# Clamp in the PSUM bank, a store in four parts, GpSimd's maxima in other places, unread TensorE products in three waits of a two-layer cross-attention kernel

## Chip, cores and metric

The kernel runs on one core of a Trainium2 chip. Its time is the device time of one execution in microseconds (us); less is better.

## What is computed

x is (16, 100, 256), the context (16, 361, 192). Four blocks each add to x what they make of layernorm(x):

```python
x = x + L0_xattn(layernorm(x), ctx)   # 16 heads of 16; scores clipped at +-1e4, softmax, PV, Wo
x = x + L0_ffn(layernorm(x))          # top-2 of 8 experts, capacity 500, plus 0.1 * a shared FFN
x = x + L1_xattn(layernorm(x), ctx)   # ternary weights, int8 activations
x = x + L1_ffn(layernorm(x))          # a recurrent cell over 16 steps
```

In L1_xattn every linear layer scales its input by the maximum of its absolute value over the whole tensor, so nothing can be multiplied before that one number is known:

```python
i_scale = jnp.maximum(jnp.max(jnp.abs(x)), 1e-08) / 127.0
qx = jnp.clip(jnp.round(x / i_scale), -128.0, 127.0)
```

There are six such maxima: of the context (CTX), of vis, the first linear layer's output (VIS), of the image embeddings (IMG_), of the normalised text (TEXT), of the concatenation (CAT) and of the hidden layer (HID).

## The kernel before

Every engine has its own stream, written out by hand in `@block.vector`, `@block.gpsimd`, `@block.scalar`, `@block.tensor` and `@block.sync` (from L2452); the order in each is fixed, and they meet by semaphores alone. There is no planner.

**Attention (L540 to L818).** `over_batches` (L988) walks 16 batches, the middle ones in a hardware loop. Each batch b has eight steps i, two heads each. TensorE (`a_tensor`, L657) issues in step i the transposed scores of batch b (L549), the plain scores of batch b + 1 (L530), and by turns the key (L378), value (L476), query (L412) and output (L621) products of other batches and the probability-value product (L577). DVE (`a_vector`, L735) takes the score maximum per query (L535), and clips the exponentials of ScalarE (L556) in L565. The maxima of eight heads at a time, a half, go to the other side of the scores as two extra rows: DVE clamps them from SBUF to SBUF (`m_vector`, L499), TensorE transposes them into a free part of bank 6 (`m_tensor`, L504), ScalarE copies the upper 16 bits out (`m_scalar`, L510), DVE the rest (`m_low`, L514), and SP stores them (L521). Half 1 of batch b is clamped and transposed in step 0, half 0 of batch b + 1 in step 4; the copies follow in steps 1 and 5, ahead of ScalarE's exponential, and there TensorE waits for L514 before L577, which writes into the same bank. In the opening, `m_vector` stands behind the maximum of i = HALF - 1 (L2475).

**Experts (L1178 to L1485).** SP stores the outputs of each expert to DRAM when its four parts are done (`expert_store`, L1480, semaphore `ys_out`): 500 KB. With the last one there, GpSimd fetches two rows per token and batch by 32 indirect transfers (L2532), and DVE adds them to x (`combine_vector`, L2111).

**Second layer (L1920 to L2211).** `lin_tensor` (L1712) makes vis and the image embeddings, evicted by ScalarE (L1735) and in part by DVE; DVE takes maxima (L1749), `quant_max` (L1585) joins them in `cmax`, GpSimd takes the maximum over the partitions (`quant_gpsimd`, L1590, PARTITION_ALL_REDUCE), and DVE turns it into scales (`quant_scale`, L1574). GpSimd has VIS's maximum behind the gathers of batch 2 (L2535). The normalised text is transposed (L210), copied to xnT by ScalarE (L2082), reduced (L2162), scaled and multiplied (L1930); then the small attention (L1763), after which CAT's maximum holds up the product L1944, and HID's the product L1977. Between these two, GpSimd prepares the recurrent cell's weights (`cell_weights_gpsimd`, L2338), the last part of them behind HID's maximum.

## Time and profile before

| | |
|---|---|
| median of 3 runs | 927.25 us (925.16 to 928.35) |
| the profiled execution | 924.2 us, of which the span from first to last instruction is 922.4 |
| busy of the span | TensorE 84%, VectorE (DVE) 77%, ScalarE (ACT) 61%, GpSimd (POOL) 33% |
| attention / experts / second layer / cell | up to about 333 / 624 / 839 / 922 us |
| mean granted TensorE clock | 0.921 of 2.4 GHz |

PE is TensorE's matmul, PEld its weight load, SPq a transfer issued by SP. Every instruction stands under the line of the kernel that issued it. "Idle before" is the time its engine stood still ahead of it, with the engine that released it as the trace infers from semaphores; "issue" means that the profile shows nothing it waited for. Buffers that share one area of SBUF (vis, image, hidden layer, text) all appear as `area`. The granted clock has two levels, 1.0 (2.4 GHz) and 0.5 (1.2 GHz); a value between them in a window is their mean over time.

### The profile page before, as it was taken

The numbers are of one execution on the slowest core, as the hardware profiler recorded it, in microseconds if no ns is written. First come the engines' busy times: TensorE is split into PE (matmuls) and PEld (weight loads), VectorE is DVE, ScalarE is ACT, GpSimd is POOL, SyncE is SP. The second block draws the span as 40 slices with busy tenths as digits, with TensorE's granted clock in tenths as the row PEclk, the third lists the DMA queues.
The fourth block names the chain that finished last, engine by engine and source line by source line (L and its number), as shares of the span: only waits on it lengthen the run. The fifth ranks groups of instructions, "written<-read, shape, count | busy, mean of one in ns | idle before, by whom it ended". The sixth has DMA issues, their size and how long they took to land.

```text
span 922.4 us, 21748 instructions
## 1 busy us (share of the span) xinstructions
PE 779.0 (84%) x8198; PEld 581.1 (63%) x8198; DVE 710.6 (77%) x1453; ACT 558.3 (61%) x1155; POOL 305.5 (33%) x254
## 2 busy tenths in 40 slices
PE   3688999999997786999899999996626999769994
PEld 2456666666665573778477777783214877459994
DVE  7779889888887896875677777637786988777766
ACT  6667677677764356443655556647957776763542
POOL 6235646555453442040522220004730221442400
PEclk9799999999999668899999999998657999889997
DMA  6434444445543447141477766521210000200002
GB/s 173 110 89 102 111 106 103 107 108 125 137 107 82 134 139 243 66 136 49 127 198 195 193 191 176 151 72 54 76 46 0 2 1 1 92 0 2 3 1 72
DMA packets 75271, 89.60 MB, mean 97 GB/s; under 512 B 22054, under 2 KB 61761, under 8 KB 75194
## 3 DMA queue, kind: packets, MB, share of 16 engines
q1 hardware_dynamic: 68362, 80.50, 31.6%
q0 software_dynamic: 6144, 7.42, 3.3%
q8 instruction: 49, 0.80, 0.4%
q10 hardware_dynamic: 688, 0.66, 0.3%
q14 instruction: 28, 0.23, 0.1%
HBM read 72.87 MB, written 15.43 MB: 96 GB/s over the span
## 4 chain that ended last, share of the span: by engine, by line
PE 47%; DVE 27%; ACT 12%; issue 8%; DMA 3%; POOL 1%; SPq 1%; DVEq 0%; another core or an unknown queue 0%; ACTq 0%
PE ps L1215 11%; PE ps L1202 9%; DVE p L565 4%; DVE m L535 3%; PE ps L378 3%; PE ps L549 3%; PE ps L476 2%; ACT area L1735 2%; PE ps L2282 2%; PE ps L577 2%; PE ps L530 2%; DVE m32c L499 2%; PE ps L2293 2%; DVE pmax L1749 1%; ACT area L2104 1%
## 5 line engine op out<-in xcount | busy, mean ns | idle before, releaser
L535 DVE TENSOR_REDUCE m<-ps 100x2 f32<-100x722 f32 x128 | 115.0, 899 | 38.6 <-PE ps L530 37.9
L556 ACT ACTIVATE p<-ps 128x800 f32<-128x800 f32 x128 | 106.8, 834 | 48.9 <-PE ps L549 46.8
L1264 ACT ACTIVATE hT<-ps,cols 128x500 f32<-128x500 f32 (+1 forms) x96 | 62.5, 651 | 99.7 <-PE ps L1202 91.5
L1271 DVE TENSOR_TENSOR hT_l<-hT,hT_h 128x500 f16<-128x500 f32 (+1 forms) x96 | 62.5, 652 | 58.6 <-ACT hT_h L1265 56.5
L1215 PE MATMUL ps<-w_h,hT_h 128*125 128x256 f16 (+1 forms) x384 | 105.0, 274 | 1.8 <-DVE x L1311 1.2
L565 DVE SCALAR_TENSOR_TENSOR p<-p 128x600 f32<-128x600 f32 x128 | 105.6, 826 | 0.7 <-ACT p L556 0.7
L1215 PE MATMUL ps<-w_h,hT_l 128*125 128x256 f16 (+1 forms) x384 | 105.0, 273 | 0.0
L1215 PE MATMUL ps<-w_l,hT_h 128*125 128x256 f16 (+1 forms) x384 | 105.0, 273 | 0.0
L1107 POOL DMA_INDIRECT xe<-tokens,slot_of x32 | 42.4, 1326 | 152.5 <-PE ps L1225 102.1
L1202 PE MATMUL ps<-xe_h,w_h 128*128 128x500 f16 (+1 forms) x192 | 72.6, 378 | 17.0 <-ACT hT_h L1265 7.2
L1202 PE MATMUL ps<-xe_l,w_h 128*128 128x500 f16 (+1 forms) x192 | 72.2, 376 | 0.0
L1202 PE MATMUL ps<-xe_h,w_l 128*128 128x500 f16 (+1 forms) x192 | 71.8, 374 | 0.0
L549 PE MATMUL ps<-qs,ks 128*128 128x100 f16 x768 | 62.8, 211 | 6.7 <-ACT p L556 4.2
L396 POOL TENSOR_TENSOR kp<-k,kp 128x361 f16<-128x361 f32 x32 | 46.0, 1437 | 62.3 <-ACT kp L392 62.3
L530 PE MATMUL ps<-ks,qs 128*100 128x361 f16 x256 | 61.8, 324 | 3.9 <-DMA qs<-q_parts 3.1
L549 PEld LDWEIGHTS ps<-qs,ks 128*128 128x128 f16 x768 | 49.9, 99 | 22.6 <-ACT p L556 10.4
L1265 ACT ACTIVATE hT_h<-ps,cols 128x500 f16<-128x500 f32 (+1 forms) x96 | 62.1, 647 | 0.0
L1215 PEld LDWEIGHTS ps<-w_h,hT_h 128*125 128x125 f16 (+1 forms) x384 | 51.1, 133 | 6.5 <-DVE hT_l L1271 1.4
L577 PE MATMUL ps<-p,v 128*32 128x100 f32 (+1 forms) x1536 | 47.9, 258 | 7.0 <-DVE mT L514 3.6
L1215 PEld LDWEIGHTS ps<-w_l,hT_h 128*125 128x125 f16 (+1 forms) x384 | 51.1, 133 | 2.7
L1215 PEld LDWEIGHTS ps<-w_h,hT_l 128*125 128x125 f16 (+1 forms) x384 | 51.1, 133 | 0.0
L577 PEld LDWEIGHTS ps<-p,v 128*32 128x32 f32 (+1 forms) x1536 | 33.7, 112 | 26.5 <-issue 11.4
(353 smaller groups left out, 2107.1 us busy)
## 6 DMA issues: line engine op xcount, KB each, us to landing
stage<-in_ctxT_dram SPq DMA_DIRECT2D x16, 541.5 KB, 6.4
sw<-in_L_ffn_w_dram SPq DMA_DIRECT2D x16, 512.0 KB
sw<-in_L_ffn_w_dram SPq DMA_DIRECT2D x8, 1024.0 KB, 6.0
k_parts<-kp SPq DMA_DIRECT2D x32, 192.0 KB, 3.3
ks<-k_parts SPq DMA_DIRECT2D x32, 192.0 KB
stage<-in_L_xattn_W_f_dram SPq DMA_DIRECT2D x6, 1024.0 KB, 7.0
ctx_f<-in_ctxT_dram SPq DMA_DIRECT2D x16, 270.8 KB, 3.2
ks<-k_parts SPq DMA_DIRECT2D x32, 96.0 KB
```

What stands on the lines that cost most here:

```text
L396: g.tensor_tensor(kp[:, 1, c, 0:KV], k32[c][:, :], kp[:, 0, c, 0:KV], ALU.subtract).then_inc(k_l, 1)
L530: mm = pe.matmul(bank[at + n][0:T, 0:KV], qs[p][:, h, :], ks[p][:, h, 0:KV], start=True, stop=True)
L535: v.tensor_reduce(m32[p][:, 2 * i:2 * i + 2], ps[0:T, at:at + 2, 0:KV], AX.X, ALU.max).then_inc(m_max, 1)
L549: mm = pe.matmul(bank[t_bank(i) + n][:, j * T:(j + 1) * T], keys, qs[p][:, h, :], start=(j == 0), stop=True, skip_group_check=True)
L556: s.activation(p32[:, i % HALF, :, :, :].rearrange("p j n t -> p n j t"), ps[:, t_bank(i):t_bank(i) + 2, 0:(KJ + 1) * T].rearrange("p n (j ...
L565: v.scalar_tensor_tensor(probs, probs, 1.0, low, ALU.min, ALU.max).then_inc(a_cv, 1)
L577: i = pe.matmul(OB_[HR * r:HR * (r + 1), g * T:(g + 1) * T], v32[p][0:m, j, h, :], p32[0:m, h // 2 % HALF, j, h % 2, :], start=(g == 0 and ...
L1202: i = pe.matmul(bank[2 + f % 2][:, 0:width(n)], w1p[ww][:, k, f * 128:(f + 1) * 128], xep[p][xx][:, k, 0:width(n)], start=(k == 0 and ww = ...
L1215: i = pe.matmul(bank[4 + j % 3][0:m, 0:C], hTp[p][hh][:, f, j * m:(j + 1) * m], w2p[of][ww][:, f, :], start=(f == 0 and hh == ww), stop=(f ...
L1264: s.activation(hT[:, f % 3, 0:m], bank[2 + f % 2][:, 0:m], ACT.Silu, bias=bias, scale=1.0 / WS)
L1265: s.activation(hTp[p][0][:, f, 0:m], bank[2 + f % 2][:, 0:m], ACT.Silu, bias=bias, scale=1.0 / WS).then_inc(f_s, 1)
L1271: v.tensor_tensor(hTp[p][1][:, f, 0:m], hT[:, f % 3, 0:m], hTp[p][0][:, f, 0:m], ALU.subtract).then_inc(f_l, 1)
```

## The change

- The clamp moves behind the transposition: TensorE transposes the maxima as they are, DVE clamps the eight rows in the bank, in place, and ScalarE waits for that. In DVE's order the clamp now stands behind the score maximum of its step. TensorE waits for the maxima and for the previous half's L514.
- The last expert's output is stored in four transfers, each when its part is done; the waits for `ys_out[1]` count them.
- GpSimd takes VIS's maximum behind the gathers of batch 4 rather than 2.
- The text maximum is taken in four parts rather than two.
- TensorE runs products that nobody reads: 10 of 512 columns in bank 0 before the text product, 18 in bank 2 after the small attention, 20 in bank 0 after L1944.
- ScalarE computes one unread Exp after the text evictions.
- GpSimd takes two unread maxima over the partitions (of TEXT's `cmax`), one ahead of CAT's and one ahead of HID's.

```diff
         def m_vector(v, b, p, half):
-            v.wait_ge(m_max, NP * b + HALF * (half + 1))
-            wait(v, m_mm, 2 * b + half)
-            v.tensor_scalar(m32c[:, :], m32[p][:, half * NP:(half + 1) * NP], CLAMP, -CLAMP, ALU.min, ALU.max
-                                   ).then_inc(m_c, 1)
-        def m_tensor(pe, b, half):
-            pe.wait_ge(m_c, 2 * b + half + 1)
-            pe.transpose(MT_, m32c[:, :], ident[0:T, 0:T]).then_inc(m_mm, 1)
+            v.wait_ge(m_mm, 2 * b + half + 1)
+            v.tensor_scalar(MT_, MT_, CLAMP, -CLAMP, ALU.min, ALU.max).then_inc(m_c, 1)
+        def m_tensor(pe, b, p, half):
+            pe.wait_ge(m_max, NP * b + HALF * (half + 1))
+            wait(pe, m_l, 2 * b + half)
+            pe.transpose(MT_, m32[p][:, half * NP:(half + 1) * NP], ident[0:T, 0:T]).then_inc(m_mm, 1)
         def m_scalar(s, b, half):
-            s.wait_ge(m_mm, 2 * b + half + 1)
+            s.wait_ge(m_c, 2 * b + half + 1)
...
         def a_vector(v, b, t, p):
             for i in range(NP):
-                if i == 0:
-                    m_vector(v, b, p, 1)
-                if i == 4 and has(b, 1):
-                    m_vector(v, b + 1, q, 0)
...
                     s_vector(v, b + 1, q, i, 2 * (i % 2))
                 else:
                     guard_flag_vector(v, i)
+                if i == 0:
+                    m_vector(v, b, p, 1)
+                if i == 4 and has(b, 1):
+                    m_vector(v, b + 1, q, 0)
...
         def expert_store(q, e, p):
+            if isinstance(e, int) and e == E - 1:
+                for j in range(4):
+                    q.wait_ge(f_y, 4 * (e + NG) + j + 1)
+                    q.dma_start(slots_y[e][:, j, :], ye[p][:, j, :]).then_inc(ys_out[p], 16)
+                return
...
+        def keep_running(pe, at, n):
+            for i in range(n):
+                pe.matmul(at, w_q[F1][:, 0, 0:128], w_q[F1][:, 1, 0:512], start=True, stop=True)
         def layer2_tensor(pe):
...
             ln_tensor(pe, 2)
+            pe.wait_ge(ln_ev, 2 * (B // 2) + 1)
+            keep_running(pe, bank[0], 10)
...
             att_tensor(pe)
+            keep_running(pe, bank[2], 18)
...
                 i.then_inc(h_mm, 1)
+            pe.wait_ge(h_ev, 8 + 4 * FC - 7)
+            keep_running(pe, bank[0], 20)
             pe.wait_ge(h_ev, 8 + 4 * FC)
...
                 if b == B // 2 - 1:
-                    s.wait_ge(ys_out[1], 16 * (E // 2 + 1))
+                    s.wait_ge(ys_out[1], 16 * (E // 2 + 4))
...
+            s.activation(avg_q[0:T, 1, 0:1], eps_col[:, :], ACT.Exp)
             s.wait_ge(pad_set, 1)
             att_scalar(s)
...
-            for h in range(2):
-                v.wait_ge(ln_ev, 2 * (B // 2) + (h + 1) * B // 4)
-                i = v.tensor_reduce(pmax[:, h:h + 1], xnT[:, :, h * NTOK // 2:(h + 1) * NTOK // 2], AX.XY, ALU.max,
-                                    apply_absolute_value=True)
+            for h in range(4):
+                v.wait_ge(ln_ev, 2 * (B // 2) + (h + 1) * B // 8)
+                i = v.tensor_reduce(pmax[:, h:h + 1], group_of(h), AX.XY, ALU.max, apply_absolute_value=True)
             vs.inc(i)
-            quant_max(v, TEXT, 2)
+            quant_max(v, TEXT, 4)
...
+            g_.partition_all_reduce(avg_q[:, 1, 2:3], cmax[:, TEXT:TEXT + 1], 128, RMAX)
             quant_gpsimd(g_, [HID])
...
-                if i == HALF - 1:
+                if i == HALF:
                     m_vector(v, 0, 0, 0)
...
-                g.wait_ge(ys_out[p], 16 * (E // 2 + 1))
+                g.wait_ge(ys_out[p], 16 * (E // 2 + 1 + 3 * p))
             for b in range(B):
...
-                if b == 2:
+                if b == 4:
                     quant_gpsimd(g, [VIS])
             quant_gpsimd(g, range(IMG_, TEXT + 1))
             att_gpsimd(g)
+            g.partition_all_reduce(avg_q[:, 1, 1:2], cmax[:, TEXT:TEXT + 1], 128, RMAX)
             quant_gpsimd(g, [CAT])
```

## Rows read from the trace of the kernel before

**Rows 1.** Windows: stretch, length, busy PE, PEld, DVE, ACT, POOL, then PEclk, DMA share, GB/s.

```profile
165.00:198.00 33.00, 31.14 (x453) 22.07 (x452) 29.34 (x43) 23.30 (x54) 19.54 (x14) 1.00 0.42 105
```

**Rows 2.** L499's own view, and the view of waits (total us, times, longest).

```profile
L499 DVE TENSOR_SCALAR m32c<-m x32: 158/800/1012, 39.8 to 299.6; 100x8 f32<-100x8 f32 x32
...
PE ps L504 <- DVE m32c L499: 13.6, 23, 2.1
```

**Rows 3.** Timeline around one clamp: start us, us, engine, line, operation, [idle before <-releaser].

```profile
211.62 1.77 POOL L650 TENSOR_TENSOR ctxl<-ctx_f,ctxh 96x361 f16<-96x361 f32 x1
...
212.37 0.47 PE L530 MATMUL ps<-ks,qs 128*100 128x361 f16 x2
...
212.58 0.84 DVE L499 TENSOR_SCALAR m32c<-m 100x8 f32<-100x8 f32 x1
...
213.48 0.25 PE L504 MATMUL ps<-const,m32c 100*8 100x100 f32 x1 [0.64 <-DVE m32c L499]
...
214.85 0.24 DVE L514 TENSOR_TENSOR mT<-ps,mT 8x100 f16<-8x100 f32 x1
...
215.35 0.72 PE L577 MATMUL ps<-p,v 128*32 128x100 f32 x24
```

**Rows 4.** Chain of waits: one product per batch (start us, us, what).

```profile
199.26 1.42 PE ps L476 x12
...
216.08 1.42 PE ps L476 x12
...
232.34 0.76 PE ps L476 x6
```

**Rows 5.** Timeline of the second layer's head: store, gathers, a maximum, ScalarE's last halt.

```profile
624.30 0.27 SPq L1482 DMA_DIRECT2D slots_out<-ye  x1
...
631.37 1.23 POOL L2532 DMA_INDIRECT xn<-slots_out,back  x1 [77.89 <-PE ps L1727]
...
641.93 0.35 POOL L1593 PARTITION_ALL_REDUCE gmax<-cmax  x1 [2.75 <-DVE cmax L1588]
...
642.46 1.04 POOL L2532 DMA_INDIRECT xn<-slots_out,back  x1 [0.17 <-issue]
...
676.49 1.07 POOL L2532 DMA_INDIRECT pick_more<-slots_out,back  x1 [0.30 <-issue]
...
679.75 0.65 ACT L1735 ACTIVATE area<-ps,cols,oscale 128x361 f32<-128x361 f32 x1 [2.03 <-PE ps L1727]
```

**Rows 6.** Timeline of GpSimd and DVE around the last two global maxima.

```profile
781.45 0.73 POOL L1996 TENSOR_TENSOR x<-x,f_b 100x256 f32<-100x256 f32 x1 [3.54 <-DVE area L1881]
...
788.58 0.15 DVE L1577 TENSOR_SCALAR iscale<-gmax 128x1 f32<-128x1 f32 x1 [3.71 <-POOL gmax L1593]
...
796.84 5.91 POOL L2344 TENSOR_SCALAR fused<-area 128x512 f16<-128x512 f32 x4 [8.29 <-issue]
...
811.46 1.48 POOL L2349 TENSOR_SCALAR area<-area 128x512 f16<-128x512 f32 x1
...
819.20 0.15 DVE L1577 TENSOR_SCALAR iscale<-gmax 128x1 f32<-128x1 f32 x1 [3.56 <-POOL gmax L1593]
```

**Rows 7.** Windows of 2 us in the second layer, columns as in rows 1.

```profile
786.00:788.00 2.00, 0.00 (x0) 0.00 (x0) 0.00 (x0) 0.00 (x0) 0.00 (x0) 0.68 0.96 320
...
792.00:794.00 2.00, 2.00 (x9) 0.94 (x8) 1.67 (x5) 1.02 (x2) 0.00 (x0) 0.61 0.08 27
...
824.00:826.00 2.00, 2.00 (x19) 2.00 (x18) 0.00 (x0) 1.98 (x3) 0.00 (x0) 0.93 0.00 0
```

**Rows 8.** Timeline of TensorE: first products after three idlings of the second layer.

```profile
699.47 5.49 PE L1930 MATMUL ps<-area,wq_txt 128*128 128x400 f16 x16 [5.46 <-ACT area L2088]
...
790.12 23.48 PE L1944 MATMUL ps<-area,wq_f 128*128 128x400 f16 x128 [6.67 <-ACT area L2100]
...
821.42 8.55 PE L1977 MATMUL ps<-wq_f,area 128*100 128x256 f16 x64 [7.81 <-ACT area L2108]
```

**Rows 9.** Timeline of DVE: the two text maxima.

```profile
693.81 3.54 DVE L2162 TENSOR_REDUCE pmax<-xnT 128x1 f32<-128x1600 f32 x2
```

More of the change, by code:

```diff
@@ L268, in build @@
         m32 = [sba(f"m32_{p}", [T, H]) for p in range(2)]
-        m32c = sba("m32c", [T, H // 2, 2])[:, :, 0]
         mT = sba("mT", [H // 2, 2, 2, T], F16)
@@ L670, in a_tensor @@
                 if i == 0:
-                    m_tensor(pe, b, 1)
+                    m_tensor(pe, b, p, 1)
                 if i == 0 and has(b, 2):
@@ L692, in a_tensor @@
                 if i == 4 and has(b, 1):
-                    m_tensor(pe, b + 1, 0)
+                    m_tensor(pe, b + 1, q, 0)
                 if i == 4 and has(b, 3):
@@ L2641, in _ @@
                 if i == HALF:
-                    m_tensor(pe, 0, 0)
+                    m_tensor(pe, 0, 0, 0)
                 if i == 0:
```

## The prediction, made before the change was run

> **What bounds the kernel now.** I read the chain that ended last first, then the stretches that it names, in time order. No engine bounds the whole; three regimes matter here. In the attention loop TensorE is busy for 31.1 of 33 us at the full clock [rows 1], so only its waits can be won. The one the change touches is that of the transpose L504 for DVE's clamp L499: 13.6 us in 23 waits [rows 2]. In the head of the second layer nothing multiplies for long, and the end of the gathers and a stuttering ScalarE set the pace [rows 5]. At its last two global maxima DVE waits 3.71 and 3.56 us for an answer of GpSimd [rows 6], while TensorE stands idle, so that its clock falls to 1.2 GHz and the next products start slowly [rows 7, 8].
>
> **The clamp.** It takes 158 ns at best, 800 as the median [rows 2]; by listing them, 18 of 32 take 0.54 us or more. A slow one ends when a GpSimd operation ends: POOL 211.62 + 1.77 = 213.39, clamp 212.58 + 0.84 = 213.42 [rows 3]. So it waits for GpSimd rather than computes. In the bank it is like L514, which takes 0.24 us with a bank as its source [rows 3]; I take 0.2. It moves behind the score maximum, and TensorE transposes unclamped maxima as soon as they are there. New dependencies: ScalarE's copy waits for that clamp, with the exponential behind it; L514 comes a clamp and a clip later, and TensorE's product L577 waits for L514.
> Slow clamp at i = 0: scores start at 212.37, L577 at 215.35, 2.98 us [rows 3]. After: 0.47 of scores; what lay between the clamp's end (213.42) and L514's end (215.09) with a maximum and a clip of DVE, 1.67; the clamp, 0.2; and some 0.2 for signals: 2.53, so 0.45 gained. At i = 4 the same sum gives 0.15 for a slow clamp and loses 0.2 for a fast one, which until now sat in idle time of DVE. With 9 slow at i = 0, 9 slow and 5 fast at i = 4: 4.05 + 1.35 - 1.0 = **4.4 us**. A cross-check: the batch with two fast clamps took 232.34 - 216.08 = 16.26 us, that with two slow ones 16.82 [rows 4], so half of the clamp's cost was hidden already. Bounds: 13.6 us [rows 2] gained; or 6 lost (32 times 0.2 ahead of the exponentials).
>
> **Stores in parts, VIS's maximum moved.** The last expert's store is issued at 624.30, the first gather starts at 631.37 [rows 5]. In parts, three quarters go out while TensorE still multiplies. Of the 7.07 us I take 5 us as data and 2 us as fixed (an estimate from that one row); a quarter leaves 3.3 us, so gathers start 3.7 us earlier, at 627.6. Ten gathers (five batches) then come before VIS's maximum instead of six. They are spaced (676.49 - 642.46) / 25 = 1.36 us. Ten end at 627.6 + 9 x 1.36 + 1.0 = 640.8, and the maximum is due at 641.93 as before [rows 5]: it fits with 1.1 to spare. Behind it 22 instead of 26 remain, so the last starts at 642.46 + 21 x 1.36 = 671.0, 5.5 us earlier. What is that worth? ScalarE halts three times in the end of this stage, last for 2.03 us before 679.75, in evictions whose products are long done; the trace blames TensorE, but the halts cease when the last gather (676.49) has landed [rows 5]. I read them as code that comes late behind the gathers, so that with gathers 5.5 us earlier the last two halts go. I take **4.3 us**: twice that 2.03, rounded up for the pieces between. Bounds: nothing (ScalarE halts anyway), and 6.7 (all three halts, 2.2 us each).
> The pages speak against the split: the Trainium skill, "DMA: Bandwidth & Descriptors", section "Rules for kernel authors", wants small transfers coalesced, as each pays about 2 us. By it alone the last part would still come 2.3 us after its issue, an estimate from that page, since the other three fixed costs lie under products.
>
> **Text maxima in four.** Two reductions take 3.54 us back to back, behind DVE's own work [rows 9], so the halves were no wait. Four cost **0.1 us more**. Bounds: 0.5 gained or lost.
>
> **TensorE runs.** Ten, eighteen and twenty products of 512 columns. At 2.4 GHz one column is 1/2.4 ns: 0.213 us each, so 2.1, 3.8 and 4.3 us; at 1.2 GHz twice that. TensorE idled 5.46 us before 699.47, 6.67 before 790.12 and 7.81 before 821.42 [rows 8]; the last two shrink by 2.35 and 1.3 (below) to 4.3 and 6.5. The runs fit: 4.3 us in 5.46 even at the low level, 3.8 in 4.3, and 4.3 in 6.5. TensorE's last product before the second idling ended at 783.45, and the clock stood at 2.4 GHz until 786.7 (0.68 over 786 to 788) [rows 7, 8]; with a run, no gap before the next products is as long as that one, so it should hold. Regained: from 821.42 to 824.28 (0.93 over 824 to 826) at half rate, **1.4 us**. From 790.12 to 793.6 (0.61) [rows 7, 8] at most 1.7, but DVE's quarters of the operand arrive one by one: **1.0 us**. Before the text product, where ScalarE's evictions set the pace, **0.3 us**. Nothing here costs more than 0.5 if a run is late.
>
> **GpSimd's maxima moved.** DVE waits 3.71 us, to 788.58, for a maximum that itself takes 0.35 [rows 5, 6]: some 3.3 us, from 784.87 on, in which GpSimd waits for nothing else. The same operation behind a gather begins at 641.93 and the next gather at 642.46 [rows 5], so there is no such time in it. So it is a change of GpSimd's code, and the change has it made by an unread maximum, issued when the last addition ends (781.45 + 0.73 = 782.2) [rows 6]. Then GpSimd is ready at 785.5, runs the unread one and the real one to 786.2 instead of 788.55: **2.35 us**. For the second, the queue ahead ends with gate weights, 811.46 + 1.48 = 812.9; these start at 796.84, 8.3 us after the maximum [rows 6], and move with it to 810.6. Plus 3.2 of code and two maxima, 814.5, against 819.2, that is 4.6 in all, of which 2.35 and 1.0 are counted: **1.3 us**. On GpSimd's queue VIS's maximum passes four gathers, as counted above; on SP's, nothing stands between the four stores but the waits for the parts. What GpSimd does behind the maxima comes earlier with them. Bounds for the pair: 5.5 gained, or 0.8 lost (each unread maximum simply in front). The extra Exp moves a table load ahead of the attention's keys, where ScalarE waits in any case, but may push the keys themselves: **0.1 us**, bounds 0.3 gained or lost.
> The Trainium skill, "GPSIMD Engine Reference", section "2.1 Instruction dispatch", gives about 6 us for a first call after new code; the trace has 3.3 [rows 6]. By the 6 of that page of the Trainium skill the unread maximum of the first pair would end at 788.6, an estimate from that page, and that pair would gain nothing.
>
> **Sum.** 4.4 + 4.3 - 0.1 + 1.4 + 1.0 + 0.3 + 2.35 + 1.3 + 0.1 = 15.1 us. The profiled execution took 924.2 us (span 922.4), so 909.1 for one like it; the runs' median is 927.25, 3 us above it, and I set the change against the median: **912 us**.
>
> **Rivals.**
> - Attention gives nothing: TensorE's wait for the clamp becomes one for L514, at the same length. For: at i = 4 my own sum nearly does that. Against: at i = 0 the transposition had TensorE idle for 0.64 us [rows 3], and L577 has 0.45 to come forward. 916.4 us; chance 0.14.
> - ScalarE's halts don't follow the gathers: the code is late by itself. Against: they end with the gathers [rows 5]. 916.3 us; 0.15.
> - A change of GpSimd's code costs more than the 3.3 us, or each maximum pays it again: the 2.35 and 1.3 go, 915.7 us. Against: the one at 641.93 [rows 5] came at once. 0.08. (The figure of the Trainium skill's "GPSIMD Engine Reference", section "2.1 Instruction dispatch", would lead here.)
> - More than thought: attention gains 9.7, more than half way from my sum to the 13.6 of [rows 2], and all halts vanish (6.7): 15.1 + 5.3 + 2.4 = 22.8, 904.4 us; 0.13.
> - It does not do what it says: the unread products leave the clock where it was, because a wait outlasts them. 914.7 us; 0.06.
> - Slower: the clamp in the bank costs 0.85 us as before, not 0.2. Its place is now between score maximum and copy, so every exponential and L577 gets 0.65 later, 32 x 0.65 = 21 us, and 4.4 goes too: 912 + 4.4 + 21 = 937. It decides from a clamp of 0.53 us on, where 32 x 0.33 eats the 10.7 that are left without 4.4. Against: L514, with the bank as source, took 0.24 in the midst of GpSimd's work [rows 3]. 0.04.
> - As forecast: 0.40.
>
> **Numbers.** What a measurement here tells from no change is 0.3%, 2.8 us. All cases but the last rival are faster by far more; for overlaps of several misses I give 0.05 to no difference. Faster 0.91, same 0.05, slower 0.04. The range takes the single misses and two together: 904 to 920.5.
>
> **What would show it.** Right: L499 uniformly near 0.2 us and no wait of L504; L577 waiting some 0.4 us for L514; first gather near 627.6, last near 671; ScalarE's halts ending near 674; GpSimd's real maxima 1.3 us after DVE's first value and 2 us after the second; granted clock 1.0 from TensorE's first run to the end of the second product. Wrong: L499 over 0.5 us; a full batch still over 16.6 us; VIS's scale later than 642.5; unread products still running when operands are ready.

## The result, and the profile after the change

The changed kernel takes 920.22 us (median of 8 runs, 915.78 to 923.52) against 927.5 us of the kernel before in the same comparison: ratio 0.9938, interval 0.9916 to 0.996. In a second comparison, with 12 runs, the ratio was 0.9959 (0.9931 to 0.9986). So the change brings 4 to 7 us, not 15. The profiled execution has a span of 916.6 us against 922.4.

Most of this study reads stretches between fixed points of the trace (start of one instruction to start of another, but from the end of the last expert product), because TensorE's stretch of expert products, which no kernel here changes, took between 276.6 and 283.4 us in the 17 executions profiled: this alone moves a whole time by 7 us. The same stretches of the kernels before and after, two executions of each, in us; "predicted" is what the prediction's terms say for the stretch, "measured" the difference of the means:

| stretch | before | after | predicted | measured |
|---|---|---|---|---|
| attention, first to last L514 | 254.94, 255.71 | 254.22, 253.97 | -4.4 | -1.2 |
| last expert product to VIS's maximum | 18.12, 18.11 | 18.12, 18.12 | 0 | 0 |
| VIS's to IMG_'s maximum | 44.51, 43.46 | 40.27, 37.97 | -4.3 | -4.9 |
| IMG_'s to TEXT's maximum | 11.19, 11.20 | 11.32, 11.31 | +0.1 | +0.1 |
| text product to CAT's maximum | 88.69, 88.46 | 88.34, 89.00 | -2.65 | +0.1 |
| CAT's maximum to product L1977 | 33.26, 33.83 | 33.87, 34.78 | -2.3 | +0.8 |
| L1977 to the cell's first product | 17.60, 18.09 | 18.23, 18.49 | -1.4 | +0.5 |
| the cell | 83.38, 83.06 | 82.91, 82.68 | 0 | -0.4 |

The attention row is smaller than the spread of single executions: ten of the traces in this study have the changed kernel's attention loop, and in them the stretch takes 253.97 to 257.9 us; three have the old one, with 254.94, 255.71 and 257.2. So attention gained nothing that the traces can show.

The attention loop first, by its full view of waits, L575 being what was L577, L512 the old L514, L497 the clamp, L377 the key product, L648 GpSimd's subtraction for `ctxl` (total us, times, longest):

```profile
PEld ps L575 <- DVE mT L512: 19.3, 24, 1.3
...
PE ps L575 <- DVE mT L512: 12.8, 24, 0.9
...
ACT mT L508 <- DVE ps L497: 11.9, 19, 1.3
...
PE ps L377 <- POOL ctxl L648: 4.0, 6, 1.3
```

Of these waits of TensorE the kernel before had

```profile
PE ps L577 <- DVE mT L514: 3.6, 11, 0.4
...
PE ps L378 <- POOL ctxl L650: 0.3, 1, 0.3
```

The clamp's own line: every one of the 32 takes 0.25 us.

```profile
L497 DVE TENSOR_SCALAR ps<-ps x32: 247/248/248, 40.5 to 298.9; 8x100 f32<-8x100 f32 x32
```

The 13.6 us that TensorE waited for the clamp [rows 2] are gone, but the wait for the lower half of the maxima has grown from 3.6 to 12.8 us, and that for `ctxl` from 0.3 to 4.0: 17.5 us in these three waits before, 16.8 in two after (and the transposition waits once for the first maxima, 1.5 us). A window of a full batch pair, columns as in rows 1:

```profile
165.00:198.00 33.00, 30.83 (x457) 22.60 (x456) 27.92 (x47) 24.04 (x56) 15.12 (x14) 1.00 0.45 106
```

TensorE is as busy as in [rows 1], 30.83 against 31.14 us; DVE and GpSimd have less to do, and ScalarE is no less busy.

The head of the second layer, GpSimd's timeline (start us, us, engine, line, operation, idle before):

```profile
625.64 1.23 POOL L2546 DMA_INDIRECT xn<-slots_out,back  x1 [74.27 <-PE ps L1730]
...
637.69 1.01 POOL L2546 DMA_INDIRECT xnT<-slots_out,back  x1 [0.30 <-issue]
639.82 0.35 POOL L1596 PARTITION_ALL_REDUCE gmax<-cmax  x1 [1.12 <-issue]
...
669.18 1.01 POOL L2546 DMA_INDIRECT pick_more<-slots_out,back  x1 [0.31 <-issue]
680.09 0.35 POOL L1596 PARTITION_ALL_REDUCE gmax<-cmax  x1 [9.90 <-DVE cmax L1591]
```

Against the last expert product (end 623.81 before, 621.70 after) the first gather comes at 3.94 instead of 7.56 us [rows 5], the last at 47.48 instead of 52.68; ten fit ahead of VIS's maximum.

The last two maxima, the timelines of GpSimd, DVE and TensorE together:

```profile
774.78 0.72 POOL L2009 TENSOR_TENSOR x<-x,f_b 100x256 f32<-100x256 f32 x1 [3.55 <-DVE area L1884]
...
776.63 4.05 PE L1926 MATMUL ps<-wq_f 128*128 128x512 f16 x18
...
778.04 0.16 DVE L1591 TENSOR_REDUCE cmax<-pmax 128x1 f32<-128x6 f32 x1
781.29 0.38 POOL L2553 PARTITION_ALL_REDUCE avg_q<-cmax  x1 [5.79 <-issue]
781.59 0.42 POOL L1596 PARTITION_ALL_REDUCE gmax<-cmax  x1
...
783.59 2.47 PE L1955 MATMUL ps<-area,wq_f 128*128 128x400 f16 x12 [2.91 <-ACT area L2114]
```

```profile
805.22 1.50 POOL L2362 TENSOR_SCALAR area<-area 128x512 f16<-128x512 f32 x1
...
806.06 4.48 PE L1926 MATMUL ps<-wq_f 128*128 128x512 f16 x20
...
807.93 0.19 DVE L1591 TENSOR_REDUCE cmax<-pmax 128x1 f32<-128x32 f32 x1
812.48 0.38 POOL L2363 PARTITION_ALL_REDUCE avg_q<-cmax  x1 [5.76 <-issue]
812.78 0.42 POOL L1596 PARTITION_ALL_REDUCE gmax<-cmax  x1
...
815.46 9.18 PE L1990 MATMUL ps<-wq_f,area 128*100 128x256 f16 x64 [4.91 <-ACT area L2122]
```

GpSimd's unread maximum starts 5.79 and 5.76 us behind the end of its last tensor operation, and that is where the real one started before: 788.16 - (781.45 + 0.73) = 5.98 and 818.79 - (811.46 + 1.48) = 5.85 us, by [rows 6] and the starts of the real maxima. The real one now starts 0.3 us behind the unread one. The granted clock in windows of 2 us (PEclk is the third number from the end):

```profile
782.00:784.00 2.00, 0.41 (x3) 0.29 (x4) 1.88 (x7) 1.51 (x2) 0.01 (x1) 1.00 0.86 283
...
812.00:814.00 2.00, 0.00 (x0) 0.00 (x0) 0.69 (x4) 0.32 (x1) 0.72 (x2) 0.69 0.00 0
...
818.00:820.00 2.00, 2.00 (x14) 1.93 (x13) 0.00 (x0) 1.98 (x3) 0.00 (x0) 0.60 0.00 0
```

At CAT the clock stays at 2.4 GHz over a gap of 2.91 us behind the unread products; [rows 7] had 0.61 in the product's first windows. At HID they end 4.91 us before the product, the clock falls to 1.2 GHz, and the product's first turn takes 9.18 us, more than the 8.55 of [rows 8].

What happened at CAT is not what the kernel does every time. In its second execution, `rep_after`, the gap was 3.06 us and the clock fell at the product's start:

```profile
780.00:782.00 2.00, 1.74 (x6) 0.84 (x7) 2.00 (x6) 1.18 (x3) 0.00 (x0) 0.53 1.04 362
782.00:784.00 2.00, 2.00 (x9) 0.92 (x8) 1.67 (x5) 1.16 (x2) 0.00 (x0) 0.61 0.09 30
```

Nine traces of this study have these runs and GpSimd's last addition ahead of CAT's maximum. The gaps at CAT are 2.61 to 3.34 us; the clock held in three (2.61, 2.82 and 2.91 us) and fell in six (2.80 to 3.34). At HID the gaps are 3.37 to 5.05 us, and it fell in all nine.

### The profile page after: what moved, and what is told of

It is laid out like the page before. It is cut to its first block, busy times and chain, and to the rows that moved or that the text cites. A ratio compares the mean times of both kernels' runs of the same rounds, so it can differ in the third digit from the quotient of the medians.

```text
span 916.6 us, 21852 instructions
## 1 busy us (share of the span) xinstructions
PE 783.5 (85%) x8246; PEld 584.2 (64%) x8246; DVE 701.6 (77%) x1455; ACT 557.9 (61%) x1156; POOL 294.8 (32%) x256
## 4 chain that ended last, share of the span: by engine, by line
PE 46%; DVE 20%; ACT 10%; issue 10%; POOL 7%; DMA 5%; SPq 1%; DVEq 0%; ACTq 0%; another core or an unknown queue 0%; POOLq 0%
PE ps L1213 11%; PE ps L1200 10%; DMA rden<-inverse 2%; PE ps L547 2%; PE ps L575 2%; ACT area L1738 2%; PE ps L475 2%; PE ps L2295 2%; PE ps L528 2%; POOL ctxl L648 2%; PE ps L2306 2%; PE ps L377 2%; DVE p L563 1%; ACT area L1705 1%; PE ps L1812 1%
## 5 line engine op out<-in xcount | busy, mean ns | idle before, releaser
L563 DVE SCALAR_TENSOR_TENSOR p<-p 128x600 f32<-128x600 f32 x128 | 105.6, 826 | 0.7 <-ACT p L554 0.7
L575 PE MATMUL ps<-p,v 128*32 128x100 f32 (+1 forms) x1536 | 47.4, 257 | 16.2 <-DVE mT L512 12.8
L395 POOL TENSOR_TENSOR kp<-k,kp 128x361 f16<-128x361 f32 x32 | 38.4, 1199 | 65.8 <-ACT kp L391 65.8
L575 PEld LDWEIGHTS ps<-p,v 128*32 128x32 f32 (+1 forms) x1536 | 33.3, 111 | 36.6 <-DVE mT L512 19.3
```

The lines of the kernel that those rows point to most:

```text
L563: v.scalar_tensor_tensor(probs, probs, 1.0, low, ALU.min, ALU.max).then_inc(a_cv, 1)
L575: i = pe.matmul(OB_[HR * r:HR * (r + 1), g * T:(g + 1) * T], v32[p][0:m, j, h, :], p32[0:m, h // 2 % HALF, j, h % 2, :], start=(g == 0 and ...
```

## The experiments

Fifteen runs, two of them the kernels before and after once more, each timed beside the kernel before in its own comparison. "The changed kernel" is the one of the diff above. Two theories of mine are tested. **Theory Q**: GpSimd's change of code begins when its queue reaches the maximum, whether or not the value is there, so the last tensor operation ahead of it sets the time. **Theory W**: in attention the wait has only changed its name, as DVE's chain of score maximum, clamp, clip and lower half releases L577. Their rivals are the steps of the prediction. Distances between two instructions are from start to start unless an end is named; "the second layer" is here all behind the last expert product, the cell included (298.6 and 298.1 us in the kernel before).

### The two kernels once more

No edit.

> The kernel before once more, for the spread of a stretch between executions. From DVE's first to its last lower half of the maxima (L514) the trace shown took 254.9 us; first expert product at 342.9. If two executions agree within 0.5 us, the 0.7 us by which that stretch is shorter after the change is real; if they differ by 2 us or more, the trace can't say whether the clamp gave 4.4 us, as predicted, or nothing, and only times can.

Measured: 924.91 us, ratio 0.9991 (0.9967 to 1.0015). Attention 255.71 us, 0.8 from the first execution.

> The changed kernel once more. The same stretch took 254.2 us. Theory W (the wait has only changed its name): again within 1 us of the kernel before. Rival (the clamp does give 4.4 us, and the trace shown was an unlucky one): 251 us or less. Of the second layer I expect the same again: GpSimd's unread maximum some 5.8 us behind its last tensor operation at both places, and the clock falling once before the second linear layer of the hidden units. Ratio 0.992 to 0.996.

Measured: 919.78 us, ratio 0.9959 (0.9931 to 0.9986); attention 253.97. The first expectation's middle case: two executions differ by about as much as the two kernels do. What is firm is a loss within the loop. From the third L514 to the ninth (three periods of the loop, called batches 1 to 4 here) the kernels before took 48.37 and 48.61 us, the changed ones 49.77 and 50.16, and all ten traces with the changed loop take 49.6 us or more: the early batches lose 1.5 us. Late ones seem to win: from the 17th to the 27th 82.61 and 83.02 against 81.87 and 82.24, but the ten traces reach from 81.6 to 82.8, so this win is within the spread. In the losing batches some GpSimd operations take far longer than before. Its timeline after:

```profile
74.21 3.10 POOL L648 TENSOR_TENSOR ctxl<-ctx_f,ctxh 96x361 f16<-96x361 f32 x1 [0.93 <-ACT ctxh L643]
...
90.51 3.33 POOL L395 TENSOR_TENSOR kp<-k,kp 128x361 f16<-128x361 f32 x1
```

and the same two before:

```profile
74.19 1.33 POOL L650 TENSOR_TENSOR ctxl<-ctx_f,ctxh 96x361 f16<-96x361 f32 x1 [0.93 <-ACT ctxh L645]
...
89.42 2.31 POOL L396 TENSOR_TENSOR kp<-k,kp 128x361 f16<-128x361 f32 x1
```

TensorE's key products wait for the `ctxl` behind it in GpSimd's queue: 1.28 and 0.27 us between 74 and 110 us, where before they waited for none. The subtraction takes 3.09 or 3.10 us in all ten traces with the changed loop. The long L395 is not needed for the loss: three of the ten have it at 0.9 us and lose as much. In other batches GpSimd is no slower than before, and its whole busy time fell from 305.5 to 294.8 us.

### The clamp

`clamp_back` restores the old clamp, its tile and its place in the order, in the changed kernel:

```diff
-            v.wait_ge(m_mm, 2 * b + half + 1)
-            v.tensor_scalar(MT_, MT_, CLAMP, -CLAMP, ALU.min, ALU.max).then_inc(m_c, 1)
+            v.wait_ge(m_max, NP * b + HALF * (half + 1))
+            wait(v, m_mm, 2 * b + half)
+            v.tensor_scalar(m32c[:, :], m32[p][:, half * NP:(half + 1) * NP], CLAMP, -CLAMP, ALU.min, ALU.max
+                                   ).then_inc(m_c, 1)
```

> The changed kernel with the clamp from SBUF to SBUF, ahead of the transposition, as before. Theory W: TensorE waits again for the clamp (some 14 us in all) in place of L514's successor, and the time is that of the changed kernel plus 0 to 1.5 us, 920 to 922 against 927.5 of before. Prediction's step: 4.4 us more than the changed kernel, 924.6. If the clamp in the bank does harm in the early batches: up to 2 us less.

Measured: 920.77 us, ratio 0.9958 (0.9939 to 0.9977), that of the changed kernel's repeat in the same comparison, 0.9959. The waits are those of the kernel before:

```profile
PE ps L504 <- DVE m32c L499: 13.4, 22, 2.2
```

The clamp's move is worth nothing that a time can show; 4.4 us would have been. With the old clamp batches 1 to 4 take 48.37 us again, and the subtraction 1.34.

`low_first` takes the lower half ahead of the clip:

```diff
                 if i == 0:
                     m_vector(v, b, p, 1)
+                    m_low(v, b, 1)
                 if i == 4 and has(b, 1):
                     m_vector(v, b + 1, q, 0)
+                    m_low(v, b + 1, 0)
```

> The changed kernel, in DVE's order the lower half of the maxima (m_low) straight behind the clamp, ahead of the clip of the exponentials. Theory W says that TensorE's product waits for DVE's chain score maximum, clamp, clip, lower half (21 waits, 11 us in all in this stretch). Then this takes out the clip, 0.77 us, of it, and most of the 11 us of waiting goes; in exchange DVE stands some 0.3 us for ScalarE's copy each time. 3 to 8 us faster than the changed kernel if TensorE sets the pace, 912 to 917; nothing, or up to 5 us slower, if DVE does.

Measured: 932.86 us, ratio 1.0097 (1.0069 to 1.0126): 13 us slower than the changed kernel, worse than either case. Its waits say why:

```profile
PE ps L575 <- DVE p L563: 33.8, 32, 2.4
...
DVE mT L512 <- ACT mT L508: 10.5, 31, 0.4
```

TensorE's product needs that clip (L563) as well as the lower half. The clip had never been a detour, and DVE's 31 halts for ScalarE now lie on the way to both. Theory W had the chain right and its cut wrong.

`no_clamp` leaves the clamp of the score maxima out of the attention loop, so large scores are no longer bounded there; ScalarE's copy waits for the transposition itself.

```diff
-            v.wait_ge(m_mm, 2 * b + half + 1)
-            v.tensor_scalar(MT_, MT_, CLAMP, -CLAMP, ALU.min, ALU.max).then_inc(m_c, 1)
+            pass
```

> The changed kernel with the clamp of the score maxima left out of the attention loop (nothing else is). It bounds what any place for the clamp can bring. Theory W: 0.25 us less in each of 27 chains if these set the pace, 912 to 916, with L577 at 2.25 us after the scores. If TensorE's other work sets it: no difference, 919. In batches 1 to 4 the changed kernel took 1.4 us more than the one before (49.8 against 48.4); if that comes from the clamp's 0.25 us it goes, if from GpSimd's operations of 3.1 to 3.3 us it stays.

Measured: 917.6 us, ratio 0.9916 (0.9891 to 0.994). From the third to the 27th L514 it takes 193.9 us, the kernels before 197.6 and 198.4, the changed ones 197.4 and 198.0. So all that any place of the clamp could give is about 4 us, and the prediction's 4.4 was the price of having no clamp at all. Batches 1 to 4 take 47.7 us, and the subtraction is short although no clamp waits beside it:

```profile
73.24 1.26 POOL L647 TENSOR_TENSOR ctxl<-ctx_f,ctxh 96x361 f16<-96x361 f32 x1 [0.92 <-ACT ctxh L642]
```

So it was not the old clamp's waiting that kept GpSimd quick.

`clamp_early` keeps the clamp in the bank but puts the transposition ahead of the step's scores on TensorE and the clamp ahead of the step's score maximum on DVE:

```diff
+                if i == 0:
+                    m_tensor(pe, b, p, 1)
+                if i == 4 and has(b, 1):
+                    m_tensor(pe, b + 1, q, 0)
                 t_tensor(pe, b, p, i)
...
-                if i == 0:
-                    m_tensor(pe, b, p, 1)
...
             for i in range(NP):
+                if i == 0:
+                    m_vector(v, b, p, 1)
+                if i == 4 and has(b, 1):
+                    m_vector(v, b + 1, q, 0)
                 if i == 1:
                     m_low(v, b, 1)
```

> The changed kernel with the transposition ahead of the step's scores on TensorE, and the clamp in the bank ahead of the step's score maximum on DVE, in time in which DVE waits for the scores anyway. Theory W: what releases L577 is DVE's chain from the scores on, score maximum, clamp, clip, lower half; with the clamp ahead of it, L577 starts 2.3 us after the scores (as with a fast clamp before), not 2.5 to 2.6: 27 times 0.2, up to 5 us less than the changed kernel. Against: TensorE now waits for the previous score maximum ahead of the exponentials' scores, which may take it back; then the batch periods stay at 16.2 to 16.6 us and the time within 1.5 us.

Measured: 918.98 us, ratio 0.9934 (0.991 to 0.9957). Batches 1 to 4 take 47.95 us, 1.8 less than in the changed kernel, and third to 27th L514 196.55, about 1.2 less. The place in DVE's chain is what had cost the early batches their time, and the subtraction takes 1.26 us here too; why the place lengthens it stays open. Of the hoped 5 us about one came in this trace and as much in that of `best` (196.36 us), while the ten traces of the changed loop reach from 197.4 to 200.3 us in the same stretch; the time is that of the changed kernel. What took the rest back, TensorE's earlier wait for instance, was not tried by itself.

### GpSimd's maxima

`no_unread_max` leaves out both unread maxima.

```diff
-            g.partition_all_reduce(avg_q[:, 1, 1:2], cmax[:, TEXT:TEXT + 1], 128, RMAX)
...
-            g_.partition_all_reduce(avg_q[:, 1, 2:3], cmax[:, TEXT:TEXT + 1], 128, RMAX)
```

> The changed kernel without GpSimd's two unread maxima. Theory Q: GpSimd's change of code begins when its queue reaches the maximum, whether or not cmax is there, and takes some 5.8 us from the end of the last tensor operation (5.98 and 5.85 us before, 5.79 and 5.76 after the change). Then the unread maxima bring nothing and cost 0.3 us each: CAT's maximum again 5.8 us behind the last addition, HID's 5.8 us behind the last gate weight, the time 0.3 to 0.9 us less. Prediction's step: 2.35 and 1.3 us lost, the time 3.6 us more.

Measured: 918.46 us, ratio 0.9937 (0.991 to 0.9963), nothing lost. GpSimd's timeline:

```profile
775.33 0.73 POOL L2009 TENSOR_TENSOR x<-x,f_b 100x256 f32<-100x256 f32 x1 [3.54 <-DVE area L1884]
781.87 0.38 POOL L1596 PARTITION_ALL_REDUCE gmax<-cmax  x1 [5.81 <-issue]
790.70 5.90 POOL L2357 TENSOR_SCALAR fused<-area 128x512 f16<-128x512 f32 x4 [8.45 <-issue]
...
805.37 1.58 POOL L2362 TENSOR_SCALAR area<-area 128x512 f16<-128x512 f32 x1
812.93 0.38 POOL L1596 PARTITION_ALL_REDUCE gmax<-cmax  x1 [5.97 <-issue]
```

The real maximum comes 5.8 and 6.0 us behind the end of the last tensor operation by itself: theory Q.

`add_behind` leaves them out too and moves the last addition to x behind CAT's maximum; `both_behind` moves the last three gate weights behind HID's as well:

```diff
+                if u < UNITS - 1:
+                    g.wait_ge(n_p, 2 * u + 2)
+                    x_b2_gpsimd(g, u)
...
             quant_gpsimd(g, [CAT])
+            g.wait_ge(n_p, 2 * UNITS)
+            x_b2_gpsimd(g, UNITS - 1)
...
+            quant_gpsimd(g_, [HID])
             for n, g in enumerate(GATES):
                 g_.wait_ge(d_half, n + 1)
                 g_.tensor_scalar(wup[g][0], wu[g], 1.0, None, ALU.mult).then_inc(d_half, 1)
-            quant_gpsimd(g_, [HID])
```

> The changed kernel without unread maxima, only the last addition to x behind CAT's maximum. Theory Q: CAT's maximum starts 0.3 us behind cmax, 3.3 us gained, and everything on GpSimd's queue behind it comes earlier by 2.6 (the addition itself, 0.72, is now in it): HID's maximum is still bound by that queue and comes 2.6 us earlier against TensorE's product of the text. So of the 7 us of the kernel with both moves this alone gives 2 to 3.3 us, and HID's maximum still starts over 3 us behind its cmax.

Measured: 917.53 us, ratio 0.9922 (0.9897 to 0.9948). CAT's maximum starts 0.30 us behind its `cmax` (3.3 to 4.0 in every kernel without the move), HID's still 4.75 us behind. CAT's maximum comes 84.5 us behind the text product, against 88.3 and 89.0 in the changed kernel: the 3.3 us that theory Q promises are there.

> The changed kernel without unread maxima, the last addition to x behind CAT's maximum and the last three gate weights (1.48 us each) behind HID's. Theory Q: CAT's change of code begins 4.3 us earlier and is over before cmax, so that its maximum starts 0.2 us behind cmax: 3.3 us gained. HID's queue ends some 7 us earlier: the maximum comes 5.5 to 7.5 us earlier in all, and with the shorter wait the clock stays at 1.0 before the second pair of layers (1 to 2 us more). Time 7 to 9 us less than the changed kernel, 911 to 913 on its scale. Rival (the change of code waits for the value, as I read it): CAT gains nothing; HID at most 4.4 us.

Measured: 913.75 us, ratio 0.9872 (0.984 to 0.9903). Its timelines:

```profile
776.74 0.38 POOL L1596 PARTITION_ALL_REDUCE gmax<-cmax  x1 [7.10 <-DVE cmax L1591]
...
792.70 6.28 POOL L2360 TENSOR_SCALAR area<-area 128x512 f32<-128x512 f32 x4
804.70 0.38 POOL L1596 PARTITION_ALL_REDUCE gmax<-cmax  x1 [5.72 <-issue]
```

```profile
801.17 4.48 PE L1927 MATMUL ps<-wq_f 128*128 128x512 f16 x20
807.33 7.16 PE L1991 MATMUL ps<-wq_f,area 128*100 128x256 f16 x64 [1.68 <-ACT area L2123]
```

At CAT GpSimd now waits for `cmax`, not the reverse. At HID GpSimd's 5.72 us still count (the maximum starts 1.4 us behind `cmax`), but TensorE's gap is 1.68 us, the clock stays at 1.0 in every window from 796 to 814, and the first turn of L1977's product takes 7.16 us instead of 9.18. The second layer takes 285.2 us against 294.9 and 294.2 of the changed kernel.

### TensorE's unread products

`no_runs` leaves out all three runs in the changed kernel, `behind_no_runs` in `both_behind`, `behind_last_run` the first two in `both_behind`.

```diff
-            pe.wait_ge(ln_ev, 2 * (B // 2) + 1)
-            keep_running(pe, bank[0], 10)
...
-            keep_running(pe, bank[2], 18)
...
-            pe.wait_ge(h_ev, 8 + 4 * FC - 7)
-            keep_running(pe, bank[0], 20)
```

> The changed kernel without TensorE's unread products. Theory Q: the clock falls before the product of the concatenation, which then ends 1 us later; but HID's maximum waits for GpSimd's queue, not for that product, so that its time moves by less than 0.3 us, and the stretch from CAT's maximum to the cell stays within 0.7 us of the changed kernel's 51.6 to 53.3. Prediction's step: 2.7 us lost in all (1.4, 1.0 and 0.3).

Measured: 919.14 us, ratio 0.9937 (0.9913 to 0.9962), the second layer 293.6 us, 0.6 less than the changed kernel's shorter one: in the changed kernel the runs bring nothing that shows.

> The kernel with the addition and the gate weights behind the maxima, without TensorE's unread products. Theory Q: with GpSimd's queue out of the way the clock shows in the time. From cmax of CAT TensorE waits some 2.5 us only, so the clock falls late or not at all there (0 to 1 us); at HID it waits some 4 us from its last product, and the second pair's first turn takes 8 to 9 us instead of 7.2. I expect 1 to 2.5 us more than with the unread products. Rival: the shorter waits alone keep the clock, and the difference is under 0.5 us in each stretch.

Measured: 917.31 us, ratio 0.9918 (0.9886 to 0.9951), and 291.2 us for the second layer, 6 more than with the runs, 5.0 of them between L1977 and the cell. The two ratios differ by 0.0046, about as much as their intervals allow for chance, so the time alone would not settle it; the trace does. More than I expected, since the clock falls before each of two turns:

```profile
808.91 8.50 PE L1986 MATMUL ps<-wq_f,area 128*100 128x256 f16 x64 [4.73 <-ACT area L2118]
```

The chain that ended last has the second turn at 8.35 us, and 6.99 in `both_behind`. It also has 2.3 us more from DVE's statistics to that second turn (7.40 against 5.14); where these come from was not looked into.

> The kernel with both moves, of TensorE's unread products only the last twenty. Without any the second layer took 291.2 us, with all 285.2. If the clock before the hidden layer's product is what counts (8.50 against 7.16 us for the first turn, 8.35 against 6.99 for the second), this has 286 to 287 us and loses 0 to 1.5 us to all three; if the eighteen before the product of the concatenation carry it, 289 to 291.

Measured: 912.79 us, ratio 0.9867 (0.9833 to 0.99), second layer 284.9 us. The clock before the product of the hidden layer carries all that shows:

```profile
805.93 4.48 PE L1927 MATMUL ps<-wq_f 128*128 128x512 f16 x20
810.82 7.16 PE L1988 MATMUL ps<-wq_f,area 128*100 128x256 f16 x64 [0.41 <-ACT area L2120]
```

The run before the product of the concatenation shortens that product (22.42 us from first to last in `both_behind`, 23.48 here), but without it HID's maximum came 25.6 us behind the product's start, with it 25.8: the time saved is spent waiting for GpSimd's queue. That too varies: in `best`, below, GpSimd was back at tensor work 7.6 us after CAT's maximum instead of 9.0, and HID's maximum came 24.4 us behind the product's start.

### The head of the second layer

`vis_back` puts VIS's maximum behind the gathers of batch 2 again, `store_whole` stores the last output in one transfer again (and sets back the counts of `ys_out`):

```diff
-                if b == 4:
+                if b == 2:
                     quant_gpsimd(g, [VIS])
```

```diff
-            if isinstance(e, int) and e == E - 1:
-                for j in range(4):
-                    q.wait_ge(f_y, 4 * (e + NG) + j + 1)
-                    q.dma_start(slots_y[e][:, j, :], ye[p][:, j, :]).then_inc(ys_out[p], 16)
-                return
```

> The changed kernel with VIS's maximum again behind the gathers of batch 2; the store stays in four parts. GpSimd then waits for cmax with 26 gathers behind it, and the last one starts some 5 us later against the last expert product than after the change (47.5 us behind it there, 52.7 before). If ScalarE's halts follow the gathers, IMG's maximum comes 4 to 6 us later (56 to 58 us behind the last expert product after the change, 61.6 to 62.6 before), the time too. Rival, the halts come by themselves: within 1 us of the changed kernel.

Measured: 924.26 us, ratio 0.9997 (0.9973 to 1.0022): all of the changed kernel's gain is gone, and the second layer takes 298.0 us, as in the kernel before. The last gather is at 52.75 us, IMG_'s maximum at 61.34 us behind the last expert product. But ScalarE never halts in this trace. GpSimd's last gather and IMG_'s maximum:

```profile
672.94 1.01 POOL L2546 DMA_INDIRECT pick_more<-slots_out,back  x1 [0.30 <-issue]
681.53 0.35 POOL L1596 PARTITION_ALL_REDUCE gmax<-cmax  x1 [7.58 <-DVE cmax L1591]
```

The maximum starts 8.6 us behind the last gather. In all eleven executions without a halt of ScalarE over 0.3 us, before and after, that distance is 8.57 to 8.77 us. ScalarE is done 52 us behind the last expert product in those with VIS's maximum at 18.1, whatever the gathers do. The repeat of the changed kernel shows DVE waiting for the gather itself, between its maxima of the image embeddings:

```profile
670.42 0.48 DVE L2138 SCALAR_TENSOR_TENSOR x<-xn,weight,x 100x256 f32<-100x256 f32 x1 [1.33 <-DMA pick_more<-slots_out,back]
```

and so does `vis_back`, 5.2 us later against the last expert product:

```profile
675.86 0.48 DVE L2138 SCALAR_TENSOR_TENSOR x<-xn,weight,x 100x256 f32<-100x256 f32 x1 [1.30 <-DMA pick_more<-slots_out,back]
```

In both IMG_'s maximum starts 5.67 us behind this addition.

> The changed kernel with the last expert's output stored in one transfer; VIS's maximum stays behind the gathers of batch 4. The first gather comes 7.5 us behind the last expert product, not 3.95, so the ten gathers end at about 21.2 us and VIS's maximum starts there, 3.3 us later than its 18.1; the last gather starts 51 us behind that product. IMG's maximum then comes 3 to 4.5 us later than the changed kernel's 56.1. So each part of this step only pays with the other.

Measured: 921.55 us, ratio 0.996 (0.9936 to 0.9984). First gather 7.61 us behind the last expert product, VIS's maximum 20.75, IMG_'s 58.77 instead of 56.1: 2.7 us, a little under the range. IMG_'s maximum, behind the last expert product, in executions without halts: 61.57 us before, 61.34 with the split alone, 58.77 with the move alone, 56.1 with both. The split is worth 0.2 us by itself and 2.7 us with the move: with VIS's maximum early, gathers that start sooner only wait at it. These are readings of traces; by the time (0.996) the kernel without the split can't be told from the changed one.

### The moves together

`best` is `both_behind` with the early clamp.

> The kernel with both moves behind the maxima (913.8 us against 925.1 in its comparison) and the transposition and clamp ahead of the step's scores. The batches 1 to 4 take 47.9 us as in the kernel with the early clamp alone, not 49.8, and the second layer the 285 us of the kernel with both moves: together 12 to 14 us less than before, ratio 0.985 to 0.988, if the two add up. If the attention's gain was spread of single executions, 0.987 to 0.990.

Measured: 911.01 us, ratio 0.9855 (0.9821 to 0.9888), batches 1 to 4 in 47.94 us and the second layer in 285.9. It is the fastest kernel here, 14.6 us under the kernel before, and beats the changed one's 0.9938 clear of both intervals. Next to `both_behind` and `behind_last_run` (0.9872 and 0.9867) it can't be told apart.

## Why the prediction was wrong

The time is within the range, 920.2 of 904 to 920.5, but the gain is half of what was forecast. Of the rivals, two happened together: attention gives nothing (0.14), and a change of GpSimd's code costs more than I took (0.08). That the time still fell inside the range speaks for the width of the range and not for the sum: by the stretches the change is worth 5.0 us, and 4.9 of them are one term, the head.

**GpSimd's maxima, 3.65 us: the step that failed worst.** I wrote "some 3.3 us, from 784.87 on, in which GpSimd waits for nothing else" and "So it is a change of GpSimd's code", and let the unread maximum start that change earlier. The 3.3 us were only the part of the change that stuck out behind `cmax`. It takes 5.7 to 6.2 us in all traces where it isn't hidden, and starts with the end of the last tensor operation. (That GpSimd loads code in this time is my reading; the traces show the time alone.) The unread maximum stood behind the same tensor operation as the real one, so it could start nothing earlier; it costs 0.3 us. The trace that says so was within reach: the last tensor operations end at 782.18 and 812.94 [rows 6], and the two maxima followed at 788.16 and 818.79, 5.98 and 5.85 us later, the same distance at two places with different waits for `cmax`. The Trainium skill, "GPSIMD Engine Reference", section "2.1 Instruction dispatch", gives about 6 us for a first call after new code; the traces agree (5.7 to 6.2 us), and I had set that figure of the Trainium skill aside for a tail of 3.3. The estimate from it, nothing for the first pair, is what came.

**The clock of the product L1977, 1.4 us: failed by the same step.** "The runs fit: [...] and 4.3 in 6.5" and "no gap before the next products is as long as that one" rested on GpSimd's answer coming early. HID's maximum came 4.85 us behind its `cmax`, the gap was 4.91 us, and the clock fell (0.69 over 812 to 814). With GpSimd's queue out of the way the same run keeps it: 7.16 us for the first turn, against 8.55 and 9.03 in the kernel before and 8.8 to 10.1 in the other traces with a late maximum of HID, whether with the runs or without. Once the queue is clear, 1.4 us was also too low a price: without the runs (`behind_no_runs`) the stretch from L1977 to the cell takes 5.0 us more, of which the two turns are 2.7. That the clock falls again before the second turn is in this trace alone; in every other one that turn takes 7.15 us.

**The clock of the product L1944, 1.0 us: right in some executions, and worthless there.** In the trace shown the stretch from its first product to HID's `cmax` went from 25.34 to 24.34 us (in the second executions from 25.95 to 25.12, with the clock fallen), but HID's maximum waits for GpSimd, whose chain (8.3 to 8.6 us back to tensor code, 16 us of weights, 5.8 us to the maximum) runs from CAT's maximum. I added up a gain on TensorE's path and one on GpSimd's at the same join.

**The clamp, 4.4 us: the sum failed, the pieces less so.** From the step's scores to L577 the average at i = 0 went from 2.77 to 2.70 us, with 2.5 to 2.6 in most batches as forecast (2.53), but 3.39 and 3.53 in two early ones; at i = 4 it rose from 2.47 to 2.58. Two readings were off without weight: the fast clamps at i = 4 are six, not five, and the L514 of [rows 3] ran while GpSimd stood idle, so that row could not show that a bank operation is free of GpSimd (the clamp in the bank, 0.25 us every time, does). The forecast priced each chain for itself and took every gain to reach the end of a batch. `no_clamp` shows the ceiling at 4 us for removing it. What the runs show in its place is a join: TensorE waits for the last of the clamp's chain, the clip and GpSimd's `ctxl`, and 17.5 us of such waits became 16.8. Also missed is that DVE's order reaches GpSimd: with the clamp behind the score maximum GpSimd's subtraction takes 3.10 us instead of 1.33, with the clamp ahead of it or left out 1.26. Which operation of DVE does this was not tried.

**The head, 4.3 us: the number near, by luck, and the reason wrong.** The counts held (first gather 3.6 us earlier, ten before VIS's maximum, the last one 5.2 earlier, all against the last expert product). "I read them as code that comes late behind the gathers" did not: ScalarE halts in six of the seventeen executions and not in the others, for a cause that no run shows, `vis_back` has none, and the gain is there all the same, because DVE adds the last gathered rows between its maxima, and IMG_'s maximum starts 8.6 us behind the last gather. The price is the gathers' own 5.2 us. The rival of the halts was half right, in its mechanism and not in its time. The two traces shown happened to have halts of 7.4 and 3.4 us, which hid this. The rule of the Trainium skill that I held against the split ("DMA: Bandwidth & Descriptors", "Rules for kernel authors") warns of transfers under 64 KB; a part here is a quarter of 500 KB, and it does not bite: the first gather follows the last product by 3.94 us in parts and by 7.61 in one.

**Small terms.** Text maxima: IMG_'s to TEXT's maximum grew by 0.1, as forecast. Text product and the unread Exp: no trace here resolves their 0.3 and 0.1.

## To carry to other kernels

Look at where an engine's queue was last busy before a late operation, not at where its input became ready: a fixed cost that starts there is removed by moving work behind the operation, never by adding a dummy in front. Before counting a gain on one engine, follow the join it runs into; two gains at one join are one. And take a second execution of the kernel before, since a halt that occurs in one trace may not be the kernel's.

## What the hardware showed that I had not expected

- GpSimd needs 5.7 to 6.2 us from its last tensor operation to a maximum over the partitions, counted from that operation's end and hidden if the value is late; and 6.7 to 9.0 us from the end of such a maximum back to tensor operations (8.60, 8.99 and 7.08 in the timelines of the changed kernel and of `both_behind`). A maximum between gathers pays neither.
- TensorE's clock stayed at 2.4 GHz over gaps of 1.68, 0.41 and 0.34 us behind unread products (HID). In nine traces of the changed order it held at CAT over gaps of 2.61, 2.82 and 2.91 us and fell in six of 2.80 to 3.34, and at HID, with 3.4 to 5.1 us, it fell in all nine. A fall costs the first turn of L1977's product 1.3 to 3.0 us (8.5 to 10.1 instead of 7.2).
- The same GpSimd subtraction, near 74 us, took 1.33 or 1.34 us with DVE's clamp from SBUF to SBUF ahead of the score maximum (three traces), 3.09 or 3.10 with the clamp in the bank behind it (ten), and 1.26 with that clamp ahead of it or with none (three).
